# One of a step's 72 gathered columns is fetched by SyncE, one DMA per pixel

## The chip, the cores and the metric

The kernel runs on one core of a Trainium2 chip. The metric is the device time of one execution in microseconds. Engines are named PE (TensorE), DVE (VectorE), ACT (ScalarE), POOL (GpSimd) and SP (SyncE).

## The reference

Input x is 4 images of 128 x 128 pixels with 64 channels, all float32. Four layers follow each other, each as x = x + layer(group_norm(x)): a 3x3 convolution with a 64x64 product; a deformable convolution; a focal modulation; a triangle product with layer norms. The change is in the second. Per group of 32 channels (2 groups) and pixel it samples 9 taps at places that the data set:

```python
offsets = conv3x3(xi, off_w[g])                    # 18 numbers for each pixel and group
loc = clip(grid + kernel_grid + offsets, 0, 127)
sampled = wa * v(y0, x0) + wb * v(y1, x0) + wc * v(y0, x1) + wd * v(y1, x1)
s = depthwise3x3(sampled) ; s = s @ pw_w[g]
```

The focal modulation's context passes through three depthwise convolutions of 3x3, 5x5 and 7x7, each followed by a gelu. The last layer is a product of two 128 x 128 matrices for each channel.

## The kernel before

**The gather.** For each image a table in DRAM holds, for every pixel and group, 128 floats (512 B): the four neighbours that a bilinear sample needs. A step treats four rows of an image; a row has 128 pixels, one for each partition, and 18 columns (2 groups x 9 taps). There are 32 steps an image and 128 in all (`STEPS`). For row r, POOL issues 18 indirect DMAs, one for each column (line 543): 128 indices of `idx` pick 128 table entries, which land in `gat[r]`. So a step has 72 gathers. Before row r POOL waits for its indices (`idx_given`) and until DVE has summed row r of the step before (`summed`), since `gat` has four buffers.

**What a step does on the others.** DVE computes the indices and weights of step n + 1 (`indices`, lines 1634 to 1652, a chain of 15 instructions), then for each row: waits until its gathers have landed (`landed[r]`), copies the row's next indices for POOL (line 1656), multiplies by the weights (line 1678), copies the next weights (line 1659), sums the four neighbours into `srow` (line 1685, `summed`). PE turns `srow` (line 1294, 1298), ACT copies it into `stt` (lines 1008, 1012), and PE makes the products of the convolution (line 1307). SP loads the offsets of the next step (line 751), stores the rows of the step before (line 757) and loads those to be added to (line 761); in image 0 it also writes twelve blocks of band matrices for the depthwise convolutions (line 610).

**The weaving.** The other layers run in the same steps, as stages. Each engine has one instruction stream, and inside a step the flows of all stages are merged by a position that each yields, 0 to `STEP` = 14; at equal positions the step's own flow comes first. Rows lie at 3r, 3r + 1 and 3r + 2 on DVE, so the sum of row 3 is at 11. A flow's own phases are scaled by 14 / (parts x phases). Nothing moves an instruction at run time: an engine that waits holds back all that is behind it.

```python
BEHIND = (Stage(("context_norm", "context_fold"), 1, 1, NORM), Stage(("context",), 2, 4, 3), Stage(("depthwise",), 8, 1, 13),
          Stage(("modulate",), 4, 2, 9), Stage(("operands_norm", "operands_fold"), 1, 1, NORM), Stage(("operands",), 4, 2, 10),
          Stage(("triangle",), 2, 4, 6), Stage(("close",), 4, 2, 11))
```

(The numbers are steps, parts in a step and phases.) Steps of image 0 carry the first layers of images 1 to 3; steps of images 1, 2 and 3 carry BEHIND for images 0, 1 and 2; BEHIND for image 3 comes after the last step, alone. SP loads or stores what the stages need, at their positions: `depthwise` its input and level 0's bands at 0, level 1's bands at 4 x 14/13, level 2's at 7 x 14/13 (lines 666, 668), each after a wait for the buffer; the mix that frees level 0's buffer is at 12 x 14/13 on DVE (lines 1541, 1542). PE's depthwise products are line 1163, their gelu on ACT is line 895. `modulate` and `close` load at 0 and 7, `operands` stores at 4.9, 6.3, 11.9 and 13.3 (line 694).

Of the kernel before, what the change touches and what calls it, by code (L numbers as in the profile page):

```python
# [22 lines left out]
F32 = mybir.dt.float32  # L23
I32 = mybir.dt.int32
U32 = mybir.dt.uint32
ALU = mybir.AluOpType
ACT = mybir.ActivationFunctionType
AX = mybir.AxisListType
ds = bass.ds

NB, H, W, C = 4, 128, 128, 64
P = 128
# [7 lines left out]
K9 = 9  # L40
G, CG = 2, 32
GK = G * K9
# [3 lines left out]
ROWS = 4  # L46
PER = H // ROWS
STEPS = NB * PER
ENTRY = 4 * CG
PAIR = 2 * CG  # L50
TABLE = W * H
# [65 lines left out]
def weave(*flows):  # L117


    times = [next(f, None) for f in flows]  # L120
    while any(t is not None for t in times):
        k = min((t, k) for k, t in enumerate(times) if t is not None)[1]
        times[k] = next(flows[k], None)


# [65 lines left out]
def build(nc, x, mats, vecs, conv_kt, conv_w, off_w, dw_w, pw_w, dw_b, gate_w, base_loc, base_idx, taps,  # L191
          out):
    ctx = ExitStack()
    with ctx:
# [60 lines left out]
        entry = loc[:, :, 0:GK]  # L255
        idxn = sb("idxn", [P, ROWS, GK], U32)
        idx = sb("idx", [P, ROWS, GK], U32)
        wtn = sb("wtn", [P, ROWS, GK, 4])
        gathered = sb("gathered", [P, ROWS, GK, ENTRY])
        gat = [gathered[:, r, :, :] for r in range(ROWS)]  # L260
# [92 lines left out]
        with nc.Block() as block:  # L353
# [80 lines left out]
        weighted, summed, turned, st_ready, rows_used, pair_added, xr_in, x2_out = sems(  # L434
            "weighted", "summed", "turned", "st_ready", "rows_used", "pair_added", "xr_in", "x2_out")
        turned_full, full_ready = sems("turned_full", "full_ready")
        (padded_c,) = sems("padded_c")
        bands_out = sems(*(f"bands_out{l}" for l in range(3)))

# [55 lines left out]
        def planes(d, b, t, par):  # L495

            return d[b].rearrange("c (h r) w -> r c h w", r=2)[par, :, ds(4 * t, 4), :]

        def half(a, par, n=C):

            return a[par * n:(par + 1) * n, :].rearrange("c (h w) -> c h w", w=W)
# [7 lines left out]
        with nc.Block() as block:  # L509

            @block.gpsimd
            def _(pool):

                def shift_upper(t):
                    nc.gpsimd.tensor_scalar(xn[C:P, 4 * t + 1:4 * t + 5, 1:W + 1],
                                            xb[C:P, t * TILE:(t + 1) * TILE].rearrange("p (h w) -> p h w", w=W),
                                            gn[C:P, 0:1], gn[C:P, 1:2], ALU.mult, ALU.add).then_inc(upper, 1)

                pool.wait_ge(gn_done, 1)
                pool.wait_ge(padded, 1)  # L520
                for t in range(TB):
                    shift_upper(t)
                pool.wait_ge(upper, TB)
                for m in range(MCH):
                    for dy in range(3):
                        for dx in range(3):
                            nc.gpsimd.tensor_scalar(wk[:, m, dx, (3 - dy) * C:(4 - dy) * C], pw[:, m, 0:C],
                                                    dw[:, m, 3 * dy + dx:3 * dy + dx + 1], None, ALU.mult)\
                                .then_inc(wk_ready, 1)
                pool.wait_ge(wk_ready, N_ZERO + MCH * K9)  # L530
                pool.wait_ge(gn_done, 2)
                for t in range(TB):
                    shift_upper(t)
                pool.wait_ge(upper, 2 * TB)

                def step(n, b):
                    for r in range(ROWS):
                        v = n * ROWS + r
                        pool.wait_ge(idx_given, v + 1)
                        pool.wait_ge(summed, v + 1)  # L540
                        pool.sem_inc(started, 1)
                        for k in range(GK):
                            nc.gpsimd.indirect_dma_start(  # L543
                                gat[r][:, k % K9 * G + k // K9, :], None, table[b].rearrange("(n e) -> n e", e=PAIR),
                                bass.IndirectOffsetOnAxis(ap=idx[:, r, k:k + 1], axis=0))\
                                .then_inc(landed[r], 16)

                for b in range(NB):
                    with pool.Fori(b * PER, (b + 1) * PER) as n:
                        step(n, b)  # L550
# [3 lines left out]
            def _(sp):  # L554
# [204 lines left out]
                def load_pairs(n):  # L759

                    sp.dma_start(xr[:].rearrange("p a w -> p (a w)"), x1[:, ds((2 * n + 1) * W, 2 * W)]).then_inc(xr_in, 16)

                def step(n, b, i):
                    yield 0
                    if not (isinstance(n, int) and n == STEPS - 1):
                        nb, ni = (b + 1, 0) if isinstance(i, int) and i == PER - 1 else (b, i + 1)
                        sp.wait_ge(off_used, n + 1)
                        load_offsets(n + 1, nb, ni)
                    for k in range(ROWS):
                        if k == 2:  # L770
                            yield 5.5
                            if not (isinstance(n, int) and n == 0):
                                store_pairs(n - 1)
                            load_pairs(n)
                        if b == 0:
                            yield 3 * k + 1
                            bands(ROWS * i + k)
                    if isinstance(n, int) and n == STEPS - 1:
                        yield STEP
                        store_pairs(n)  # L780
# [588 lines left out]
            def _(dve):  # L1369
# [247 lines left out]
                def indices(n):  # L1617

                    count = [0]

                    def then(ins):

                        count[0] += 1
                        ins.then_inc(chain, 1)
                        dve.wait_ge(chain, CHAIN * n + count[0])

                    def xy(a, c):
                        return a[:].rearrange("p r (k c) -> p r k c", c=2)[:, :, :, c]

                    def groups(a):  # L1630
                        return a.rearrange("p r (g k) -> p r g k", g=G)

                    dve.wait_ge(off_in, 16 * n + 16)
                    tt(loc[:], off[:], base[:], ALU.add).then_inc(off_used, 1)  # L1634
                    dve.wait_ge(off_used, n + 1)
                    then(ts(loc[:], loc[:], 0.0, float(W - 1), ALU.max, ALU.min))
                    then(nc.vector.tensor_copy(inti, loc[:]))
                    then(nc.vector.tensor_copy(whole[:], inti))

                    then(tt(w_lo[:], whole[:], loc[:], ALU.is_gt))  # L1640
                    then(tt(whole[:], whole[:], w_lo[:], ALU.subtract))
                    then(tt(w_hi[:], loc[:], whole[:], ALU.subtract))
                    then(ts(w_lo[:], whole[:], 1.0, float(W - 1), ALU.add, ALU.min))
                    then(tt(w_lo[:], w_lo[:], loc[:], ALU.subtract))
                    for cx, wx in enumerate((w_lo, w_hi)):
                        for cy, wy in enumerate((w_lo, w_hi)):
                            then(tt(wtn[:, :, :, 2 * cy + cx].rearrange("p r (k g) -> p r g k", g=G),  # L1647
                                    groups(xy(wx, 0)), groups(xy(wy, 1)), ALU.mult))
                    then(nc.vector.scalar_tensor_tensor(entry, xy(whole, 0), float(H), xy(whole, 1),
                                                        ALU.mult, ALU.add))  # L1650
                    then(tt(idxn[:], entry, gbase[:], ALU.add))
                    then(ts(xy(base, 1), xy(base, 1), float(ROWS), None, ALU.add))
                    assert count[0] == CHAIN

# [13 lines left out]
                def row(n, r, give):  # L1668

                    v = n * ROWS + r  # L1670
                    yield 3 * r
                    dve.wait_ge(landed[r], 16 * GK * (n + 1))
                    if give:
                        give_indices(v, r)
                    dve.wait_ge(wt_given, v + 1)
                    g4 = gat[r][:].rearrange("p k (q c) -> p k q c", q=4)
                    wb = wt[:, r, :, :].unsqueeze(3).to_broadcast([P, GK, 4, CG])
                    tt(g4, g4, wb, ALU.mult).then_inc(weighted, 1)  # L1678
                    yield 3 * r + 1
                    dve.wait_ge(weighted, v + 1)  # L1680
                    if give:
                        give_weights(v, r)
                    yield 3 * r + 2
                    dve.wait_ge(turned, v + 1)
                    nc.vector.tensor_reduce(srow[r % 2][:].rearrange("p (s c) -> p s c", c=CG),  # L1685
                                            gat[r][:].rearrange("p s (q c) -> p s c q", q=4), AX.X, ALU.add)\
                        .then_inc(summed, 1)
# [163 lines left out]
```

## Time and profile before

| | us |
|---|---|
| timed runs, median of 3 | 12372.07 |
| timed runs, lowest and highest | 12347.44, 12374.3 |
| profiled execution, span from first to last instruction | 17350.5 |
| POOL busy with gathers in the profiled execution | 8708.9 |
| DVE, PE, ACT busy in it | 5165.4, 8037.3, 1769.5 |

The profiled execution is an execution of its own, and its time is its span: it is much longer than the timed ones, which carry no profiler. A line of the profile such as L543 is a line of the kernel. "Idle before" is the time in which the engine did nothing ahead of these instructions, and after the arrow stands who ended it; "issue" means that nothing in the profile did. SPq and POOLq are issues of DMAs.

### The profile page before, as it was taken

Reading aid. Unit: us, or ns where it says so; the run is one execution under the profiler, and the core shown is the slowest. Engines: PE = TensorE matmul, PEld = TensorE weight load, DVE = VectorE, ACT = ScalarE, POOL = GpSimd, SP = SyncE. Lnnn points to the kernel's source line nnn. Section 1 sums busy time; section 2 is a strip of 40 time slices with the busy share of each in tenths; the row PEclk is TensorE's granted clock in tenths of the full one; section 3 lists DMA queues with packets and bytes.
Section 4 is the critical chain, followed back from the end, with each engine's and each line's share of the span. In section 5 each row is a group of like instructions: output and inputs, shape, how many; then the busy total and the mean of one; then the engine's idle time right before and its main releaser. Section 6 shows DMA issues by size and latency. Waiting matters only on the chain.

```text
span 17350.5 us, 102336 instructions
## 1 busy us (share of the span) xinstructions
PE 8037.3 (46%) x30934; PEld 5581.5 (32%) x30934; DVE 5165.4 (30%) x5993; ACT 1769.5 (10%) x2822; POOL 8759.5 (50%) x9300
## 2 busy tenths in 40 slices
PE   4444444445345544443335555344325555443358
PEld 2223223223234432232224443232223443222245
DVE  2222222322333233233222233223223223222323
ACT  1001101110000011100000001110000001110014
POOL 4555555455554555455554455555555444545530
PEclk7667677667667776666667777666667777666679
DMA  2222222222223321222123321222112332122233
GB/s 78 68 60 66 78 62 70 72 61 77 61 75 98 98 60 48 63 80 59 43 61 99 98 84 45 57 77 68 46 52 77 98 98 61 48 64 77 60 124 118
DMA packets 878203, 1254.74 MB, mean 72 GB/s; under 512 B 183384, under 2 KB 663064, under 8 KB 859992
## 3 DMA queue, kind: packets, MB, share of 16 engines
q0 software_dynamic: 294912, 604.57, 13.7%
q1 hardware_dynamic: 511784, 596.71, 10.7%
q10 hardware_dynamic: 71344, 51.39, 0.9%
q8 instruction: 89, 1.46, 0.0%
q14 instruction: 74, 0.61, 0.0%
HBM read 1069.42 MB, written 245.43 MB: 76 GB/s over the span
## 4 chain that ended last, share of the span: by engine, by line
another core or an unknown queue 40%; PE 20%; issue 19%; DVE 10%; ACT 3%; PEldq 2%; PEld 1%; SPq 1%; DMA 1%; ACTq 1%; DVEq 1%
PE acc L1307 8%; PE stage L1163 6%; DVE srow L1685 5%; PE stage L1035 2%; PEldq L483 2%; DVE gathered L1678 2%; PE pt L1294 1%; ACT stt L1008 1%; PEld acc L1307 1%; PE stage L1102 1%; PE stage L1081 1%; DMA off<-offs 1%; DVE wtn L1647 0%; SPq L694 0%
## 5 line engine op out<-in xcount | busy, mean ns | idle before, releaser
L543 POOL DMA_INDIRECT gathered<-table,idx x9216 | 8708.9, 945 | 7844.0 <-issue 4412.7
L1307 PE MATMUL acc<-stt,room 128*128 128x256 f32 (+2 forms) x15360 | 4368.5, 438 | 4763.0 <-ACT stt L1008 2491.7
L1307 PEld LDWEIGHTS acc<-stt,room 128*128 128x128 f32 (+1 forms) x15360 | 3242.4, 221 | 5803.8 <-issue 2728.6
L1685 DVE TENSOR_REDUCE srow<-gathered 128x576 f32<-128x2304 f32 x512 | 2097.1, 4096 | 324.7 <-remote 207.2
L1163 PE MATMUL stage<-room 128*128 128x128 f32 x6784 | 1035.3, 303 | 1067.5 <-issue 1049.5
L1163 PEld LDWEIGHTS stage<-room 128*128 128x128 f32 x6784 | 962.5, 218 | 1139.8 <-issue 1134.0
L1678 DVE TENSOR_TENSOR gathered<-gathered,wtb 128x2304 f32<-128x2304 f32 x512 | 1304.4, 2548 | 1.2 <-issue 1.2
L1008 ACT ACTIVATE stt<-pt 128x1024 f32<-128x1024 f32 (+1 forms) x512 | 415.6, 812 | 8375.5 <-remote 4988.2
L1666 DVE SCALAR_TENSOR_TENSOR xs<-acc,fused,xr 128x256 f32<-128x256 f32 x128 | 61.7, 482 | 3747.9 <-PE acc L1307 2206.0
L1035 PE MATMUL stage<-room,mat 128*128 128x512 f32 (+1 forms) x1360 | 776.2, 694 | 841.1 <-issue 338.9
L1294 PE MATMUL pt<-mat,srow 128*128 128x128 f32 x2048 | 427.2, 337 | 1475.6 <-DVE srow L1685 1250.7
L1294 PEld LDWEIGHTS pt<-mat,srow 128*128 128x128 f32 x2048 | 283.6, 170 | 1731.5 <-DVE srow L1685 1358.7
L1035 PEld LDWEIGHTS stage<-room,mat 128*128 128x128 f32 x1360 | 275.5, 229 | 1174.8 <-issue 618.6
L1634 DVE TENSOR_TENSOR loc<-off,base 128x144 f32<-128x144 f32 x128 | 39.0, 305 | 1351.2 <-DMA off<-offs 1225.7
L1102 PE MATMUL stage<-room,offw 128*72 (+1 forms) x768 | 387.7, 655 | 97.2 <-PEq L483 57.4
L1012 ACT ACTIVATE stt<-pt 64x256 f32<-64x256 f32 (+1 forms) x512 | 166.3, 325 | 2531.9 <-remote 1357.2
L1081 PE MATMUL stage<-room,cw 128*128 (+1 forms) x768 | 368.9, 636 | 50.3 <-PEq L483 44.9
L1600 DVE TENSOR_TENSOR room<-stage,room 128x512 f32<-128x512 f32 x56 | 36.5, 687 | 946.0 <-ACT room L915 936.1
L1575 DVE SCALAR_TENSOR_TENSOR room<-stage,moved_by,room 128x512 f32<-128x512 f32 x56 | 39.8, 747 | 773.3 <-ACT room L915 740.3
L1535 DVE TENSOR_REDUCE room<-room 128x4 f32<-128x512 f32 x64 | 44.0, 687 | 732.8 <-ACT room L895 732.8
L1035 PE MATMUL stage<-room,scaled 128*128 x336 | 230.4, 790 | 55.3 <-PEq L483 33.8
L1439 DVE SCALAR_TENSOR_TENSOR room<-stage,fused,room 128x512 f32 (+1 forms) x64 | 48.0, 750 | 659.6 <-remote 444.0
(212 smaller groups left out, 4575.2 us busy)
## 6 DMA issues: line engine op xcount, KB each, us to landing
gathered<-table,idx POOLq DMA_INDIRECT x9216
room<-toep SPq DMA_DIRECT2D x48, 1792.0 KB, 7.0
room<-toep SPq DMA_DIRECT2D x64, 1280.0 KB, 8.0
room<-toep SPq DMA_DIRECT2D x64, 768.0 KB
table<-room SPq DMA_DIRECT2D x64, 512.0 KB
toep<-in_taps SPq DMA_DIRECT2D x128, 224.0 KB
gathered<-toep SPq DMA_DIRECT2D x16, 1792.0 KB, 7.0
toep<-in_taps SPq DMA_DIRECT2D x128, 160.0 KB
```

The source lines that it names most:

```text
L483: eng.drain().then_inc(met, 1)
L543: nc.gpsimd.indirect_dma_start(gat[r][:, k % K9 * G + k // K9, :], None, table[b].rearrange("(n e) -> n e", e=PAIR), bass.IndirectOffsetOn ...
L1008: nc.scalar.activation(stt[:, SLOT_OF[r], 0:4, 1:W + 1], over_slots(r, pt[:]), ACT.Copy)\
L1012: nc.scalar.activation(stt[0:C, SLOT_OF[r], 4, 1:W + 1], over_slots(r, pt[0:C, 0, :]), ACT.Copy)\
L1035: return nc.tensor.matmul(dst, w, r, start=True, stop=True)
L1081: ins = nc.tensor.matmul(PB[u][:], cw0[:, 2 * k:2 * k + 2, :].rearrange("p a c -> p (a c)"), window(k // 3, k % 3, t), start=(k == 0), sto ...
L1102: ins = nc.tensor.matmul(PB[0][0:2 * NOFF, :], offw[:, k, :], window(k // 3, k % 3, t), start=(k == 0), stop=(k == 5))
L1163: ins = nc.tensor.matmul(PB[2 * u + l % 2][:, c * W:(c + 1) * W], band(b, l, u)[:, c * k + dx, :], cin[l][u][:, c, at:at + W], start=(dx = ...
L1294: ins = nc.tensor.transpose(pt[:, m, :], srow[r % 2][:, m * P:(m + 1) * P], M["ident"])
L1307: ins = nc.tensor.matmul(sums_of[:, pairs, :], wk[0:kk, m, dx, at:at + P], stt[0:kk, slots, m, dx:dx + W], start=start and m == 0 and dx == 0,
L1678: tt(g4, g4, wb, ALU.mult).then_inc(weighted, 1)
L1685: nc.vector.tensor_reduce(srow[r % 2][:].rearrange("p (s c) -> p s c", c=CG), gat[r][:].rearrange("p s (q c) -> p s c q", q=4), AX.X, ALU. ...
```

## The change

DVE computes for column 17 of row 3 (`FETCHED`) the byte address of each pixel's entry in the table, as integers in a column `pixel_at` (one more tensor_scalar in `indices`, which before it waits until SP's DMA of the step has read the last one). POOL gathers 17 columns for row 3, 18 for the others. SP, in a flow of its own merged into its step at positions 0.5 to 4.0: waits for the addresses, issues a DMA that turns the column of 128 addresses into a row on one partition, waits for it, waits until row 3 of the step before has been summed, and then eight times loads sixteen addresses into registers and issues sixteen DMAs of 512 B, each with a start from a register, to one partition each. DVE waits for all 128 before it uses row 3. Three semaphores of the setup serve again for these waits.

```diff
+FETCHED = (3, GK - 1)
+CHUNK = 16
+def merged(*flows):
+    times = [next(f, None) for f in flows]
+    while any(t is not None for t in times):
+        t, k = min((t, k) for k, t in enumerate(times) if t is not None)
+        yield t
+        times[k] = next(flows[k], None)
...
+        pixel_at = sb("pixel_at", [P, 1], I32)
+        pixel_row = sb("pixel_row", [1, P], I32)
...
+        pixels_given, pixel_row_in, pixels_in = composed, x_in[1], x_in[2]
+        GIVEN0, ROW0, PIXELS0 = 2, 16, 16
...
-                        for k in range(GK):
+                        for k in range(gathered_by_pool(r)):
...
+                def fetch(n, b, at):
+                    r, k = FETCHED
+                    slot = k % K9 * G + k // K9
+                    source = table[b].bitcast(U8)
+                    yield at
+                    sp.wait_ge(pixels_given, GIVEN0 + n + 1)
+                    sp.dma_start(pixel_row[:], pixel_at[:]).then_inc(pixel_row_in, 16)
+                    sp.wait_ge(pixel_row_in, ROW0 + 16 * n + 16)
+                    sp.sem_inc(started, 1)
+                    sp.wait_ge(summed, ROWS * n + r + 1)
+                    sp.sem_inc(started, 1)
+                    for first in range(0, P, CHUNK):
+                        yield at + 4 * first / P
+                        _, starts = nc.values_load_multi_w_load_instructions(
+                            pixel_row[:, first:first + CHUNK], engines=[mybir.EngineType.SP], min_val=0,
+                            max_val=4 * PAIR * (G * TABLE - 1),
+                            skip_runtime_bounds_check_because="the coordinates are clipped to the image")
+                        for p, start in enumerate(starts, first):
+                            sp.dma_start(gat[r][p:p + 1, slot, :].bitcast(U8), source[ds(start, 4 * ENTRY)].unsqueeze(0))\
+                                .then_inc(pixels_in, 16)
+
                 def step(n, b, i):
+                    return merged(step_body(n, b, i), fetch(n, b, 0.5))
+
+                def step_body(n, b, i):
...
+                    dve.wait_ge(pixel_row_in, ROW0 + 16 * n)
+                    ts(pixel_at[:], entry[:, FETCHED[0], FETCHED[1]:FETCHED[1] + 1], 4.0 * PAIR,
+                       4.0 * PAIR * TABLE * (FETCHED[1] // K9), ALU.mult, ALU.add).then_inc(pixels_given, 1)
...
-                    dve.wait_ge(landed[r], 16 * GK * (n + 1))
+                    dve.wait_ge(landed[r], 16 * gathered_by_pool(r) * (n + 1))
+                    if r == FETCHED[0]:
+                        dve.wait_ge(pixels_in, PIXELS0 + 16 * P * (n + 1))
```

## Rows read from the trace of the kernel before

**Rows 1.** The page: span and DMA packets.
```profile
span 17350.5 us, 102336 instructions
...
DMA packets 878203, 1254.74 MB, mean 72 GB/s; under 512 B 183384, under 2 KB 663064, under 8 KB 859992
```

**Rows 2.** Groups of POOL: busy us, mean ns, then idle before, and who ended it.
```profile
L543 POOL DMA_INDIRECT gathered<-table,idx x9216 | 8708.9, 945 | 7844.0 <-issue 4412.7 <-DVE idx L1656 2511.3 <-DVE srow L1685 920.0
```

**Rows 3.** Timeline of POOL, first and last gathers: start us, us, then what.
```profile
181.27 1.16 POOL L543 DMA_INDIRECT gathered<-table,idx  x1 [33.74 <-DVE idx L1656]
182.73 0.94 POOL L543 DMA_INDIRECT gathered<-table,idx  x1 [0.30 <-issue]
183.98 0.94 POOL L543 DMA_INDIRECT gathered<-table,idx  x1 [0.30 <-issue]
185.23 0.94 POOL L543 DMA_INDIRECT gathered<-table,idx  x1 [0.30 <-issue]
...
16699.52 0.94 POOL L543 DMA_INDIRECT gathered<-table,idx  x1 [0.30 <-issue]
```

**Rows 4.** Timeline in depthwise steps: POOL's wait, and single matmuls of PE.
```profile
5288.91 0.95 POOL L543 DMA_INDIRECT gathered<-table,idx  x1 [34.57 <-DVE idx L1656]
...
5358.69 0.37 PE L1163 MATMUL stage<-room 128*128 128x128 f32 x1 [1.83 <-issue]
5361.49 0.37 PE L1163 MATMUL stage<-room 128*128 128x128 f32 x1 [2.43 <-issue]
5363.59 0.37 PE L1163 MATMUL stage<-room 128*128 128x128 f32 x1 [1.73 <-issue]
```

**Rows 5.** Timeline of one depthwise step, from level 1's products on.
```profile
5272.70 9.10 PE L1163 MATMUL stage<-room 128*128 128x128 f32 x80
5277.50 4.81 SPq L668 DMA_DIRECT2D room<-toep  x2
5283.99 4.13 DVE L1685 TENSOR_REDUCE srow<-gathered 128x576 f32<-128x2304 f32 x1
5291.85 7.92 PE L1163 MATMUL stage<-room 128*128 128x128 f32 x62
...
5314.26 5.58 PE L1163 MATMUL stage<-room 128*128 128x128 f32 x34 [0.33 <-issue]
5322.63 4.11 DVE L1685 TENSOR_REDUCE srow<-gathered 128x576 f32<-128x2304 f32 x1
```

**Rows 6.** Timeline of SP alone, where the next step's level 0 begins.
```profile
5330.22 0.40 SPq L666 DMA_DIRECT2D room<-ctxd  x1
5330.81 0.36 SPq L668 DMA_DIRECT2D room<-toep  x1
5331.66 0.40 SPq L666 DMA_DIRECT2D room<-ctxd  x1
5332.25 0.36 SPq L668 DMA_DIRECT2D room<-toep  x1
```

**Rows 7.** Single source lines: count, duration in ns min/median/max, first and last start.
```profile
L565 SPq DMA_DIRECT2D table<-zero x4: 292/293/338, 37.7 to 3177.0; - x4
...
L668 SPq FUSED_REGOPS  x192: 37/43/43, 5063.0 to 17026.7; - x192
L668 SPq MOVE room<-toep x176: 20/29/38, 5063.1 to 17014.2; - x176
...
L694 SPq DMA_DIRECT2D b_d<-room x128: 3/690/1592, 6868.4 to 17238.1; - x128
...
L1652 DVE TENSOR_SCALAR base<-base x128: 199/201/235, 174.2 to 16549.1; 128x72 f32<-128x72 f32 x128
```

**Rows 8.** The page's DMA issues: count, KB each, median us from issue to landing.
```profile
room<-toep SPq DMA_DIRECT2D x48, 1792.0 KB, 7.0
room<-toep SPq DMA_DIRECT2D x64, 1280.0 KB, 8.0
...
b_d<-room SPq DMA_DIRECT2D x128, 128.0 KB, 2.4
...
room<-gated SPq DMA_DIRECT2D x4, 256.0 KB, 2.8
```

More of the change, by code:

```diff
@@ L25 @@
 U32 = mybir.dt.uint32
+U8 = mybir.dt.uint8
 ALU = mybir.AluOpType
@@ L497, in planes, with gathered_by_pool @@
             return d[b].rearrange("c (h r) w -> r c h w", r=2)[par, :, ds(4 * t, 4), :]
+        def gathered_by_pool(r):
+            return GK - 1 if r == FETCHED[0] else GK
         def half(a, par, n=C):
```

## The prediction

> **What bounds the kernel now.** I read the page first [rows 1]. It says 17350.5 us for the profiled execution, yet the median of the timed runs is 12372.07 us: profiling stretches this kernel by 40%, so no share of that span can be taken over as it stands. The group of POOL's gathers comes next [rows 2]: 9216 of them, 8708.9 us busy and 7844.0 us idle between, over half of the idle put down to "issue". The timeline of POOL says which part is the kernel's: one gather follows the other every 1.25 us (182.73, 183.98, 185.23), the first starts at 181.27, the last at 16699.52, ending at 16700.46 [rows 3]. With 9216 gathers back to back, 9216 x 1.249 = 11511 us, the 181 us ahead of the first and the 17350.5 - 16700.5 = 650 us behind the last, the sum is 12342 us. That is 30 us (0.24%) from the median. So in the timed runs POOL issues gathers almost without a pause, and its pauses in the profile belong to the stretched execution. The timeline of PE shows the stretching: single matmuls of 0.37 us that start 2.1 and 2.8 us apart while nothing but "issue" precedes them, where the same group otherwise runs at 80 in 9.10 us [rows 4, 5]; in the same stage POOL waits 34.57 us for DVE to give it indices [rows 4]. I therefore take durations and distances from stretches without such gaps, and make the sum on the median, through the 12342 us above.
>
> The step is 72 gathers, 72 x 1.249 = 89.9 us. Every other engine has spare time in it, but DVE, PE, ACT and SP each follow one fixed order, and rows hand over in a ring of four buffers: POOL may refill row r only when DVE has summed row r of the step before.
>
> **The gain.** POOL issues 71 gathers a step: 128 x 1.249 = 160 us less, all on the path. The step becomes 71 x 1.249 = 88.7 us.
>
> **What SP takes on.** Per step: a DMA that turns the column into a row and a wait for it, a wait for DVE's sum of row 3 of the previous step, then 8 times one load of sixteen registers and 16 DMAs.
> *The DMA.* SP's one DMA on one partition, table<-zero, takes 0.292 us [rows 7]. A DMA with an address from registers has a MOVE (29 ns) and a FUSED_REGOPS (43 ns) ahead of it [rows 7]; between the end of one issue, 5330.62, and the start of the next, 5330.81, lie 0.19 us for both and the gaps around them, some 0.04 each [rows 6]. Both make a pitch of 0.292 + 0.19 = 0.482 us. The start here is already a byte address, so I take the MOVE and leave out the arithmetic with its gap, 0.08: 0.402. With neither it is 0.342, the lower bound.
> *The register load.* No row shows one. Below lies a MOVE, 0.03 us; above a small load from HBM until it has landed, 2.8 us [rows 8]. I take 0.8, nearer to a memory trip without HBM.
> The fetch F is 128 x 0.402 + 8 x 0.8 = 57.9 us; its bounds are 44.0 (0.342, 0.03) and 84.1 (0.482, 2.8).
> The Trainium skill, "DMA: Bandwidth & Descriptors", section "Latency and other measured facts", puts the floor of a load from memory into a register at about 600 ns. No row here shows it; by it an estimate of F would be 56.3 and the sum below 34 us lower.
> *DVE.* One more tensor_scalar on 128x1 each step; the nearest, on 128x72, is L1652 at 0.2 us [rows 7]. 128 x 0.2 = 26 us on an engine that is not on the path: nothing. It also waits for SP's row DMA of the same step, issued just behind the load of offsets for which DVE's indices wait anyway; 15 chained instructions lie in between, so nothing.
> *DMA engines.* 16,384 packets of 512 B beside 878203 [rows 1]: nothing for bandwidth.
>
> **Where the fetch lies.** SP's positions for its chunks are 0.5 to 4.0 of 14, so whatever the stages ask of SP later than 4.0 stands behind all 128 DMAs, and the fetch itself can't start before DVE has summed row 3. In plain steps this is covered: row 3 is summed some 10 us after POOL's last gather (landing 2.4, products 2.55, sum 4.1 and two copies), the fetch ends at 10 + 3 + 58 = 71, under 88.7. Stages that need SP after position 4 add, by the rows of their issues (0.69 us for a b_d store, landing 2.4 [rows 7, 8]), 10 to 25 us: operands' 16 stores a step are the worst, 58 + 25 = 83. Still covered.
>
> Not covered is **depthwise** (8 steps for each of images 0 to 2, 24 in all). Its three levels are a chain through SP: level 1's bands are issued at 4 x 14/13 = 4.3, just behind the fetch, level 2's at 7.5, and DVE sums row 3 (position 11) behind level 2's products (10.8). From the end of the fetch, by the timeline of one such step [rows 5, 6]:
> - level 1's bands: 0.1 + 8.0 landing [rows 8] = 8.1
> - PE level 1, 80 matmuls: 9.1, at 17.2
> - until level 2's matmuls start (gate, sum of row 2, turn, products): 5281.80 to 5291.85 = 10.05, at 27.3. Level 2's bands (issued at 5277.50 in the middle of PE's level 1, landing 7.0 [rows 5, 8]) land by then
> - PE level 2, 7/5 x 80 = 112 matmuls at 9.10/80 = 0.114: 12.8, at 40.1 (the 28 us of the profile hold the stretching)
> - until the sum of row 3 starts: 5319.84 to 5322.63 = 2.8, at 42.9; it ends at 47.0
> - from that start to SP's fourth issue of level 0 of the next step: 5322.63 to 5332.61 = 10.0, at 52.9 (SP waits there for the mix, which comes after the sum)
> - the row DMA, 0.4 + 2.4: at 55.7, and the next fetch begins.
> A depthwise step thus takes F + 55.7 = 113.6 us, 24.9 over POOL's 88.7. Before, the same chain from level 0's loads closed in some 66 us (8.1, 48 matmuls in 5.5, and 52.9), under 89.9.
>
> *What the ring absorbs.* Let T be POOL's end of a step. In the first depthwise step the fetch starts about 15 us after the previous T, ends at 73, and row 3 is summed at 73 + 47 = 120, that is T + 31. POOL wants that buffer at T + 3 x 22.5 = T + 67: 36 us in hand. The other seven steps lose 24.9 each. POOL stalls 7 x 24.9 - 36 = 138 us per image, 414 in three.
>
> **The sum.** 12372 - 160 + 414 = 12626 us (+2.1%). Against the profiled execution's own parts it is 12342 + 254 = 12596 plus the same 30.
>
> **Rivals.**
> *1. The fetch stays hidden.* In depthwise the chain behind it would have to be shorter in a timed run than the rows of the stretched execution make it: POOL doesn't stall as long as 7e is below 36, a step of 93.9 us, a chain of 36 instead of 55.7. Then only the gain is left, 12212 us; the two cancel at a step of 101.5 (3 x (7 x 12.8 - 36) = 160). For it: my distances come from a profile that is 40% slow. Against: the parts are durations of single groups without gaps and landings of 7 to 8 us. With F at its lower bound too, 44.0, the step is 99.7 and the time 12334.
> *2. The fetch is longer, and all steps become SP's.* With arithmetic and a load of 1.4 us F is 73: depthwise 128.8, stalling 244 per image, and the others at F + 20 = 93, 4.3 over in 104 steps: 12212 + 732 + 447 = 13391. At 84.1 it is 14780. For it: no row shows a load, and the dynamic issues of L668 carry both register instructions. Against: the addresses need no scaling.
> *3. One DMA engine can't follow.* Completions of one DMA after the other on the same engine are shown every 0.8 us (stores of 0.69 us each, landing in 2.4 [rows 7, 8]), not every 0.4. If a DMA took 0.8 us there, F would be 102, and with 122 us a step the time 12212 + 128 x 33 + 24 x 36 = 17300. The Trainium skill, same page, section "Why a DMA increments its semaphore by 16 and not by 1", says that a DMA on one partition runs on one engine, the lowest-numbered, so all 128 would queue at the same one; no row shows this either way.
> *4. POOL isn't the bound.* Then 160 us aren't to be had; the 0.24% of the sum above speaks against it, and the stall would come on top all the same (12786).
>
> **Chances and range.** Forecast (depthwise alone pays, F 51.7 to 68.1, 12500 to 12840, with rival 4): 0.60. Rival 2 up to 13500: 0.18. Above that (rivals 2 and 3): 0.07. Rival 1: 0.11. F at its lower bound, within 35 us of the time before: 0.04. The range leaves out rival 1 and the tail above: 12340 to 13500; the forecast's own is 12500 to 12840. A measurement of this kernel can tell about 0.2%, 25 us. Faster 0.12, same 0.03, slower 0.85.
>
> **What would show it.** POOL 9088 gathers. SP some 16,500 DMAs more, in every step a dense stretch of 128 that begins after DVE's sum of row 3; their pitch tests 0.402, the gap every sixteenth tests 0.8. In depthwise, PE's level 1 waits for bands issued behind the last fetch, and POOL waits for DVE's sum at row 3 above all, step by step about 114 us; in modulate and plain steps it has no such wait. A pitch under 0.30 us, or level 1's bands issued in the middle of the fetch, would make me wrong on one side; a load of several us or landings that pile up behind the issues on the other. The profile's own span is no measure, since some 49,000 more records on SP stretch it further.

## The result and the profile after

The changed kernel takes 12642.52 us (median of 4 runs, 12630.99 to 12646.0), the kernel before 12373.18 us: ratio 1.0218, 95% interval 1.0203 to 1.0232. The forecast was 12626.

The head of the page of the changed kernel and its group of gathers (as [rows 1, 2]):

```profile
span 12640.0 us, 137171 instructions
...
DMA packets 925614, 1257.38 MB, mean 99 GB/s; under 512 B 216152, under 2 KB 712216, under 8 KB 907096
...
L564 POOL DMA_INDIRECT gathered<-table,idx x9088 | 8622.0, 949 | 3244.5 <-issue 3206.9
```

This profile is not stretched: its span is the timed duration. Where [rows 2] hid the kernel behind pauses, here the idle time can be read. Of the 3206.9 us put down to "issue", 0.30 us ahead of each gather is the normal distance and the rest are pauses. The same group with no fetch at all (experiment 1 below) has 2768.1 us; the difference, 438.8 us, is time in which POOL stood still. Then the account closes: the first gather starts at 180.76, 9088 gathers at a mean of 1.2538 us from one start to the next (pauses left out) make 11394.8, with the pauses they end at 12013.4, and 626.6 us follow. Gathers saved: 128 x 1.25 = 160. Lost: 438. Net +278, measured +269.

The pauses lie where depthwise runs. DVE's timeline and POOL's behind it, in the third of the first image's eight depthwise steps on DVE; POOL is a step ahead and stands before row 2 of the fourth:

```profile
3803.82 4.13 DVE L1736 TENSOR_REDUCE srow<-gathered 128x576 f32<-128x2304 f32 x1
...
3808.74 0.94 POOL L564 DMA_INDIRECT gathered<-table,idx  x1 [23.17 <-issue]
```

POOL has idled 23.17 us when it resumes, less than a microsecond after DVE's sum ends at 3807.95, although the profile calls it "issue": the wait belongs to POOL's sequencer, and the releaser isn't recognised. The sum is that of row 2, and all the long pauses lie ahead of row 2: 22.4 to 23.8 us in six steps of each of the three images. Pauses of 0.7 to 5.0 us stand in these steps and the ones beside them, and there are none elsewhere but for the 33.94 us at the start.

What DVE had waited for is in the timeline of the step before, the second depthwise one. First SP alone, then PE, ACT and DVE (as [rows 5, 6]):

```profile
3667.87 3.76 SPq L803 DMA_DIRECT2D gathered<-table  x12
3671.91 0.93 SPq L689 DMA_DIRECT2D room<-toep  x2
3673.06 0.36 SPq L778 DMA_DIRECT2D x<-xs  x1
3673.62 0.41 SPq L782 DMA_DIRECT2D xr<-x  x1
3684.82 4.81 SPq L689 DMA_DIRECT2D room<-toep  x2
3690.29 0.34 SPq L772 DMA_DIRECT2D off<-offs  x1
3721.37 0.40 SPq L687 DMA_DIRECT2D room<-ctxd  x1
...
3723.40 0.37 SPq L689 DMA_DIRECT2D room<-toep  x1
3723.88 0.49 SPq L791 DMA_DIRECT2D pixel_row<-pixel_at  x1
3732.87 2.24 SPq L803 DMA_DIRECT2D gathered<-table  x7
```

```profile
3677.76 11.35 PE L1209 MATMUL stage<-room 128*128 128x128 f32 x80 [30.58 <-DMA room<-toep]
3691.30 4.12 DVE L1736 TENSOR_REDUCE srow<-gathered 128x576 f32<-128x2304 f32 x1
3698.34 12.67 PE L1209 MATMUL stage<-room 128*128 128x128 f32 x112
3711.04 0.60 ACT L941 ACTIVATE room<-stage 128x512 f32<-128x512 f32 x1 [5.65 <-PE stage L1209]
3713.79 4.11 DVE L1736 TENSOR_REDUCE srow<-gathered 128x576 f32<-128x2304 f32 x1
...
3731.50 0.15 DVE L1699 TENSOR_SCALAR pixel_at<-loc 128x1 int32<-128x1 f32 x1 [3.73 <-DMA pixel_row<-pixel_at]
```

The last of 128 pixel DMAs is followed at once by level 1's bands (3671.91), for which PE had waited 30.58 us. From there the chain runs through level 1, level 2, the sums of row 2 (3691.30, between the two levels) and row 3 (3713.79) and the next step's level 0. The next step's bands of level 1 come 112 us later.

The fetch itself, by its source lines (count, then ns min/median/max):

```profile
L803 SPq MOVE gathered<-table x16384: 29/29/39, 195.3 to 11985.4; - x200
L803 SPq DMA_DIRECT2D gathered<-table x16384: 217/228/382, 195.4 to 11985.5; - x200
...
L798 SPq TENSOR_LOAD <-pixel_row x1024: 1133/1231/2222, 194.1 to 11979.3; - x171
```

One MOVE and one DMA a pixel, no arithmetic. Twelve in 3.76 us (above) are a pitch of (3.76 - 0.23) / 11 = 0.321 us.

### The profile page after: what moved, and what is told of

The parts are those of the page before. It is cut to its first block and busy times, and to the rows that moved or that the text cites. A ratio compares the mean times of both kernels' runs of the same rounds, so it can differ in the third digit from the quotient of the medians.

```text
span 12640.0 us, 137171 instructions
## 1 busy us (share of the span) xinstructions
PE 7605.8 (60%) x30934; PEld 5399.9 (43%) x30934; DVE 5176.5 (41%) x6121; ACT 1779.0 (14%) x2822; POOL 8672.8 (69%) x9172
## 5 line engine op out<-in xcount | busy, mean ns | idle before, releaser
L564 POOL DMA_INDIRECT gathered<-table,idx x9088 | 8622.0, 949 | 3244.5 <-issue 3206.9
L1353 PE MATMUL acc<-stt,room 128*128 128x256 f32 (+2 forms) x15360 | 4100.6, 421 | 315.2 <-ACT stt L1054 315.2
L1353 PEld LDWEIGHTS acc<-stt,room 128*128 128x128 f32 (+1 forms) x15360 | 3121.7, 212 | 1223.7 <-issue 385.0
L1705 DVE COPY idx<-idxn 128x18 uint32<-128x18 uint32 x512 | 98.3, 192 | 3202.9 <-DMA gathered<-table,idx 2786.9
L1209 PE MATMUL stage<-room 128*128 128x128 f32 x6784 | 866.8, 295 | 762.9 <-DMA room<-toep 759.9
L1209 PEld LDWEIGHTS stage<-room 128*128 128x128 f32 x6784 | 859.6, 211 | 782.7 <-issue 779.6
L1582 DVE TENSOR_TENSOR room<-room 128x512 f32<-128x512 f32 x128 | 88.1, 688 | 980.5 <-ACT room L941 980.4
L941 ACT ACTIVATE room<-stage 128x512 f32<-128x512 f32 x192 | 115.3, 601 | 1455.7 <-PE stage L1209 1455.4
L1127 PEld LDWEIGHTS stage<-room,cw 128*128 128x128 f32 x768 | 150.0, 200 | 225.4 <-issue 224.4
L1148 PEld LDWEIGHTS stage<-room,offw 128*72 128x72 f32 x768 | 115.1, 158 | 269.6 <-issue 258.9
```

The costliest lines, as they stand in the source:

```text
L564: nc.gpsimd.indirect_dma_start(gat[r][:, k % K9 * G + k // K9, :], None, table[b].rearrange("(n e) -> n e", e=PAIR), bass.IndirectOffsetOn ...
L941: nc.scalar.activation(dst, PB[2 * u + l % 2][:].rearrange("p (c w) -> p c w", w=W), ACT.Gelu).then_inc(gelu_s[u], 1)
L1127: ins = nc.tensor.matmul(PB[u][:], cw0[:, 2 * k:2 * k + 2, :].rearrange("p a c -> p (a c)"), window(k // 3, k % 3, t), start=(k == 0), sto ...
L1148: ins = nc.tensor.matmul(PB[0][0:2 * NOFF, :], offw[:, k, :], window(k // 3, k % 3, t), start=(k == 0), stop=(k == 5))
L1209: ins = nc.tensor.matmul(PB[2 * u + l % 2][:, c * W:(c + 1) * W], band(b, l, u)[:, c * k + dx, :], cin[l][u][:, c, at:at + W], start=(dx = ...
L1353: ins = nc.tensor.matmul(sums_of[:, pairs, :], wk[0:kk, m, dx, at:at + P], stt[0:kk, slots, m, dx:dx + W], start=start and m == 0 and dx == 0,
```

## The experiments

The experiments start from the changed kernel, except 9. Idle time put down to "issue" in POOL's group, less the 2768.1 us of experiment 1, is called the stall. The groups ran on different chips: the kernel before took 12354.6 us beside experiments 1 to 4 and 12375.4 beside 5 to 8, against 12373.2 beside the changed kernel. Where 20 us matter, times of different groups are compared by their distance from it.

**1. No fetch.**

```diff
-                    return merged(step_body(n, b, i), fetch(n, b, 0.5))
+                    return step_body(n, b, i)
...
-                    if r == FETCHED[0]:
-                        dve.wait_ge(pixels_in, PIXELS0 + 16 * P * (n + 1))
```

The column is set to zero once, in the setup, and DVE's wait for SP's row DMA goes too, with the row DMA itself.

> Leaves out: SP fetches no pixel, so the last column of row 3 keeps what it held; POOL still issues 71 gathers. Theory (all the loss is POOL's stall in the depthwise steps, behind SP's fetch): 12642 less the 438 us of POOL's stalls seen in the trace of the changed kernel = 12204 us, 169 under the kernel before. Rival (71 gathers save less than 160 us because POOL is not the bound, and DVE's added instruction and the rest cost the difference): 12300 or more.

Measured 12192.96 us, ratio to the kernel before 0.9868 (0.9852 to 0.9885).

```profile
POOL gathered L564 <- issue: 2768.1, 9085, 0.3
...
POOL gathered L564 <- DVE idx L1704: 34.6, 3, 33.9
```

(Total us, times, longest us.) No pause is longer than 0.3 us, but for the one at the start. The gain of the 128 gathers is real and whole: 12354.6 - 12193.0 = 162 us on that chip. The changed kernel is 450 us slower; 19 of them lie between the chips, as the kernel before shows, and 431 come with the fetch.

**2 and 3. Fewer pixels.** 64, then 96 of the 128 are fetched (the rest of the column is set to zero once, in the setup).

```diff
-                    for first in range(0, P, CHUNK):
+                    for first in range(0, 64, CHUNK):
...
-                        dve.wait_ge(pixels_in, PIXELS0 + 16 * P * (n + 1))
+                        dve.wait_ge(pixels_in, PIXELS0 + 16 * 64 * (n + 1))
```

> Leaves out: SP fetches 64 of the 128 pixels. The fetch is 26 us instead of 52, a depthwise step 112.6 - 26 = 86.6 us, under POOL's 88.7. Theory: no stall, 12204 us, as with no fetch. Rival (each pixel's DMA costs time by itself, by traffic or on the one DMA engine): the loss is in proportion to the pixels, 12204 + 219 = 12423 us.

Measured 12199.4 us (12195.96 to 12202.5), 6 us above no fetch.

> Leaves out: SP fetches 96 of the 128 pixels. The fetch is 39 us, a depthwise step 99.6 us; per image the stall of 146 us falls by 7 x 13 = 91 to 55. Theory: 12204 + 165 = 12369 us, the time of the kernel before. Rival in proportion to the pixels: 12204 + 329 = 12533 us.

Measured 12306.25 us (12291.52 to 12320.64), stall 122 us:

```profile
POOL gathered L564 <- issue: 2890.1, 9078, 12.1
```

Half of the pixels costs 6 us, three quarters 113, all 431. That is the bent line of a fetch that has cover and then outgrows it; a price for each DMA would give 216 and 323. At 64 pixels the expectation was 5 us off, at 96 it was 63 us too high. Of these, 43 are stall, 122 and not 165: the expectation shortened seven steps by 13 us, but the first depthwise step is shorter too and adds to what the ring absorbs. 146 less eight times 13 gives 42 an image, 126 in all. The other 19 or so lie between the chips, since the expectation started from the 12642 us of another one.

**4. The same fetch, spread.**

```diff
-                        yield at + 4 * first / P
+                        yield at + 9 * first / P
```

> The eight chunks lie at positions 0.5 to 8.4 instead of 0.5 to 4.0, all 128 pixels fetched: level 1's bands are issued after four chunks, level 2's after seven. By the distances in the trace of the changed kernel a depthwise step is 26 (four chunks) + 30 (three chunks, stores, level 2's landing) + 12.7 + 2.8 + 10 + 7.5 (row DMA) = 89 us. Theory (the order on SP is what costs): POOL hardly stalls, 12204 to 12225 us. Rival (the fetch as such, its issues and traffic, costs the time): 12642 us, as the work is the same.

Measured 12229.09 us, ratio to the kernel before 0.9897 (0.988 to 0.9913). SP in a depthwise step:

```profile
3719.89 24.70 SPq L803 DMA_DIRECT2D gathered<-table  x64
3744.87 0.94 SPq L689 DMA_DIRECT2D room<-toep  x2
3747.11 5.15 SPq L803 DMA_DIRECT2D gathered<-table  x16
3752.48 0.39 SPq L778 DMA_DIRECT2D x<-xs  x1
3753.07 0.37 SPq L782 DMA_DIRECT2D xr<-x  x1
3754.83 11.76 SPq L803 DMA_DIRECT2D gathered<-table  x32
3766.86 0.94 SPq L689 DMA_DIRECT2D room<-toep  x2
3769.10 5.32 SPq L803 DMA_DIRECT2D gathered<-table  x16
```

Level 1's bands go out behind 64 pixels, level 2's behind 112. All 16384 DMAs are there, and 395 of the 431 us are gone (by the distance from the kernel before): the place in SP's order was the cost, not the work. What is left of stall, (2775.7 - 2768.1) + (62.2 - 34.6) = 35 us, counting also the waits for indices, lies in image 0 but for 2 us at the start of image 1, none of it in depthwise.

**5. The row DMA ahead of the step.**

```diff
-                    yield at
+                    yield -0.1
                     sp.wait_ge(pixels_given, GIVEN0 + n + 1)
                     sp.dma_start(pixel_row[:], pixel_at[:]).then_inc(pixel_row_in, 16)
+                    yield at
                     sp.wait_ge(pixel_row_in, ROW0 + 16 * n + 16)
```

> The DMA that turns the column into a row is issued ahead of everything else of the step (its addresses are there since the step before); the wait for it stays where it was. In depthwise steps it takes 7.5 us behind level 0's bands, in others 2 to 3. Theory: a depthwise step falls from 112.6 to 105, the stall per image from 146 to 93, the time to 12642 - 158 = 12485 us. Rival (the landing is covered by something else, such as the wait for the sum): 12642 us.

Measured 12483.16 us (ratio to before 1.0086, 1.0069 to 1.0103), stall 278 us; 159 us less than the changed kernel, 157 expected. Between the last issue of level 0 and the first pixel DMA there are now 2.2 us instead of 9.5:

```profile
3814.25 0.36 SPq L689 DMA_DIRECT2D room<-toep  x1
3816.44 50.86 SPq L804 DMA_DIRECT2D gathered<-table  x128
```

**6. Four bytes of each pixel.** The column is set to zero once, in the setup.

```diff
-                            sp.dma_start(gat[r][p:p + 1, slot, :].bitcast(U8), source[ds(start, 4 * ENTRY)].unsqueeze(0))\
+                            sp.dma_start(gat[r][p:p + 1, slot, 0:1].bitcast(U8), source[ds(start, 4)].unsqueeze(0))\
```

> Leaves out: of each pixel's 512 bytes SP fetches the first 4; the number of DMAs and registers is the same. Theory (SP's issue time is the cost): 0.32 us a DMA as before, 12642 us. Rival (bytes, or the one DMA engine on which all 128 run, make the fetch long): faster, down to 12204 us.

Measured 12640.33 us (12620.34 to 12656.34), stall 438 us as before. The bytes don't count. The number of DMAs is the same, so this run doesn't tell whether the engine that carries them keeps up; their landings do (rival 3 below).

**7. Loads of eight.** `CHUNK = 8`.

> Sixteen register loads of eight values instead of eight of sixteen. If a load costs by the instruction (1.23 us), the fetch is 9.8 us longer, a depthwise step 122.4, the stall per image 146 + 7 x 9.8 = 215, the time 12642 + 206 = 12848 us, with image 0's steps near POOL's 88.7 too. If it costs by the value (0.077 us each): 12642 us.

Measured 12733.45 us (12730.35 to 12735.12), stall 529 us. Neither price was right; the load costs both ways:

```profile
L798 SPq TENSOR_LOAD <-pixel_row x2048: 683/783/1740, 195.5 to 12074.6; - x187
```

Eight values 0.783 us, sixteen 1.231: 0.335 us plus 0.056 for each value. The fetch becomes 16 x 0.783 - 8 x 1.231 = 2.7 us longer by the loads and 3.7 by its ends in the trace; the gaps around each load and the first DMA behind it (0.263 us, not 0.228) add the rest. In 24 depthwise steps, the first of each image included, 3.7 make 89 us; 91 were measured.

**8. Both of 4 and 5.**

> Chunks at 0.5 to 8.4 and the row DMA ahead of the step, both. A depthwise step is 82 us by the distances above. Theory: POOL does not stall, 12204 us, as with no fetch at all and at least as fast as the spread alone. Rival (the fetch costs something of its own beside its place): over 12240 us.

Measured 12226.81 us, ratio to the kernel before 0.988 (0.9863 to 0.9896).

```profile
L564 POOL DMA_INDIRECT gathered<-table,idx x9088 | 8644.3, 951 | 2806.5 <-issue 2770.4
```

The stall is 2 us: all 128 pixels are fetched and POOL never waits for it. This version is 149 us faster than the kernel before and 416 faster than the changed one. It was expected 23 us faster still. Against experiment 1 the gathers themselves are 31 us longer (8644.3 busy against 8613.0). Some 16 of these are spread evenly over all 128 steps, and this chip is 21 us slower with the kernel before too; the other 15 lie in the depthwise steps, where a gather takes 0.972 us on the mean against 0.961. By the distance from the kernel before, the fetch in its best place costs 13 us (149 saved against 162), which the overlapping intervals of the two ratios don't tell from nothing.

**9. The kernel before, profiled once more.**

> The kernel before, profiled once more. Theory of the prediction: its first profile, 17350.5 us, was stretched by the profiling and its timed runs are POOL's gathers back to back. An unstretched profile has a span near the timed 12372 us, gathers 1.25 us apart throughout, and no wait of POOL for DVE beyond the first. Rival (profiling always stretches this kernel): a span of some 17000 us again.

It took 12356.03 us, and so did the profile:

```profile
core 0: 12354.2 us, clock 0.771
```

```profile
POOL gathered L543 <- issue: 2805.1, 9204, 0.3
...
POOL gathered L543 <- DVE idx L1656: 34.8, 4, 33.8
```

The stretching of [rows 1 to 4] was of that one profiled execution, and unstretched POOL's only real pause is the one of the start.

## Why the prediction was right

**POOL bounds the kernel.** Shown by experiments 1 and 9. Reading 9216 gathers at 1.249 us out of a stretched profile gave 12342 for 12373, and the saving of 160 is 162. The 12342 is nearer than its parts: in experiment 9's profile the gathers take 11545 us, not 11511, and 627 follow the last, not 650. Rival 4 is out.

**Only depthwise pays.** Shown: POOL's pauses lie there alone, and experiment 4, which changes only where SP issues, takes them away. The other stages stayed under POOL's pace, as said. One sign was named wrongly: POOL was to wait at row 3 above all, and it waits at row 2. Level 1's bands hold back both sums, which lie 22.5 us apart (they end at 3695.42 and 3717.90), the time of 18 gathers, so POOL meets row 2's first and finds row 3's ready or nearly so.

**The length of a depthwise step.** Predicted F + 55.7 = 113.6, found 112.8 on the mean. The terms beneath are less good than the sum, and their misses cancel, which is luck:

| term | predicted | found |
|---|---|---|
| DMA pitch | 0.402 | 0.321 |
| load of sixteen | 0.8 | 1.23 |
| fetch F, first load to end | 57.9 | 52 |
| bands landed, PE level 1 starts | 8.1 | 6.1 |
| PE level 1 done | 17.2 | 17.5 |
| level 2 starts | 27.3 | 26.7 |
| level 2 done | 40.1 | 39.4 |
| sum of row 3 starts | 42.9 | 42.1 |
| SP's level 0 issues done | 52.9 | 52.1 |
| row DMA landed, next fetch begins | 55.7 | 60.0 |

(Found, from the end of the last pixel DMA, 3671.64: 3677.76, 3689.11, 3698.34, 3711.01, 3713.79, 3723.77; the next fetch's first load starts 1.2 us before the DMA at 3732.87. From level 1's bands on, the rows are counted from the end of the fetch.) The DMA's price was taken from the nearest row, 0.292 us, and is 0.228. The row DMA was taken at 2.8 us, by the landing of a b_d store; behind level 0's four loads the next fetch begins only 7.9 us after their issue. Experiment 5 shows that those microseconds were on the path: with this term alone put right, 5.1 us more in 21 steps, the forecast would have been some 90 us too high, and with F alone put right, 5.8 us less, some 140 too low.

**The ring's reserve.** Predicted 138 us of stall per image and 414 in all, found 146 and 438. Here too two misses cancel. Seven steps of 112.8 over POOL's own 89.0 lose 167, where 174 was forecast; but the ring absorbs only 20 of them, not 36. The first depthwise fetch was to start 15 us after POOL's end of the step before. It starts 34 us after it in the first image (3468.20 to 3502.48), and 36 in the others, so row 3 is summed 47 us after POOL's next end, not 31. SP's timeline ahead of this fetch:

```profile
3460.29 25.02 SPq L663 DMA_DIRECT2D ctxd<-room  x12
3490.92 0.44 SPq L670 DMA_DIRECT2D room<-gated  x1
...
3494.66 1.00 SPq L791 DMA_DIRECT2D pixel_row<-pixel_at  x1
3503.72 5.14 SPq L803 DMA_DIRECT2D gathered<-table  x16
```

The twelve stores of the context stage stand ahead of it in SP's order, behind them SP waits until 3490.92, then come level 0's loads, and the row DMA again takes some 8 us. The prediction left this stage's end out. So the mechanism and the place were right, and the closeness of 12626 to 12643 owes much to misses that offset each other.

**The rivals.** Rival 1 is out for the changed kernel: the chain behind the fetch is 60 us, not 36. Its price of 12212 us is what is nearly reached when the fetch moves (12229 and 12227), for another reason than the one that it gave. Rival 2: the load was dearer than thought, but not by enough, and there is no arithmetic. Rival 3: experiment 2 and the landings exclude it. By the trace's semaphore updates the last pixel of a fetch has landed 1.2 us after SP's last issue (median of the steps, at most 1.7), so with a DMA every 0.321 us nothing piles up; the fetch takes 52 us and not 102.

The Trainium skill (DMA: Bandwidth & Descriptors, section "Why a DMA increments its semaphore by 16 and not by 1"), which the prediction cites for one engine, has that number go by the dimensions of the pattern, and by whether software splits a contiguous row. Here each pixel's DMA made one data packet, of 512 B (128 in the trace's packets for the fetch of the second depthwise step), which speaks for one engine each; on which one, the trace doesn't tell. The floor of a load into a register is about 0.6 us by the Trainium skill (DMA: Bandwidth & Descriptors, section "Latency and other measured facts"). The trace agrees: the shortest load of eight took 0.683 us, the median 0.783, and the median load of sixteen 1.231.

The profile was to be stretched further by some 49,000 more records. It wasn't: with 137171 instructions against 102336 it spans 12640.0 us.

## What to carry to other kernels

An engine that only issues DMAs can have much idle time, and its order is a path all the same: what is put into it delays all that stands behind, and the price is read at the stage whose loads come next, not at the average. Here 52 us of work a step cost the kernel 431 us in one piece, and 36 us or less when it was cut so that the loads that others wait for went out in between (experiments 4 and 8). A small DMA whose result the next instruction needs is better issued ahead of the large transfers of its queue: that alone gave 159 us (experiment 5).

## What was not expected of the hardware

- One profiled execution of the kernel before took 17350.5 us, another 12354.2; timed ones agree within 0.3%. Why the first was stretched stays open.
- A small DMA between two SBUF tiles (512 bytes in all) landed some 7.5 us after its issue behind level 0's four loads (two of bands, two of context). Experiment 5 moved it ahead of them and saved about that.
- A register load from SBUF takes 0.335 us and 0.056 for each value, by the line through the medians of the two sizes tried.
- The gather runs at one of two speeds. In the profiles of the kernel before (both), of experiments 1 to 4 and of 6 most gathers take 943 to 944 ns on the mean and follow each other at 1.248 to 1.249 us; in those of the changed kernel and of experiments 5, 7 and 8 it is 946 ns and 1.251 us. Experiments 5 to 8 ran on one chip, and 6 fetches no less often than the others, so it looks like a thing of the execution and not of the kernel. Over 9088 gathers it makes some 23 us, near the spread of timed runs of one kernel (12620 to 12656 us in experiment 6). What sets it stays open.
